# A two-layer decoder on one core: causal maxima and turned rows of maxima leave the place between a step's two pairs of scores

## What is computed

```
scale = 1.0 / sqrt(16)
q = heads(x @ Wq + bq);  k = heads(x @ Wk + bk);  v = heads(x @ Wv + bv)
att = where(causal, einsum('bhqd,bhkd->bhqk', q, k) * scale, -inf)
y = einsum('bhqk,bhkd->bhqd', softmax(att), v)
qc = heads(x @ Wcq + bcq);  kc = heads(ctx @ Wck + bck);  vc = heads(ctx @ Wcv + bcv)
y = y + einsum('bhqk,bhkd->bhqd', softmax(einsum('bhqd,bhkd->bhqk', qc, kc) * scale), vc)
return y @ Wp + bp
```

## Time and profile before

| | |
|---|---|
| time, median of 3 runs | 1605.59 us (1604.62 to 1607.55) |
| span of the profiled execution, first to last instruction | 1608.6 us |
| PE busy | 1504.9 us, 94% of the span |
| DVE, ACT, POOL busy | 871.6, 712.0, 571.8 us |
| steps of `xa` | 301 to 585 us |
| steps of `a1` | 889 to 1030 us |
| steps of `a2` | 1147 to 1380 us |

### The profile page before, as it was taken

The page is one execution under the profiler, slowest core; times in us unless marked ns, Lnnn a source line. Parts: engine busy times, 40 slices in busy tenths (PEclk is TensorE's granted clock), DMA queues, the critical chain, the costliest instruction groups (busy, mean ns, idle before and its releaser), DMA issues.

```text
span 1608.6 us, 24316 instructions
## 1 busy us (share of the span) xinstructions
PE 1504.9 (94%) x9774; PEld 818.2 (51%) x9774; DVE 871.6 (54%) x1838; ACT 712.0 (44%) x1035; POOL 571.8 (36%) x637
## 2 busy tenths in 40 slices
PE   7999999999999996997899999998899999998997
PEld 4678863333333353694553333564233333567997
DVE  3256538888888636204673567435677775213221
ACT  4544323366656644432334455443355556432331
POOL 3043225622222211403021355431367778613211
PEclk9999999999999998999999799999799999998999
DMA  6000020000000007972300000130200000190200
GB/s 208 1 1 1 1 50 7 1 1 1 1 1 1 1 1 261 318 246 62 40 21 1 1 1 2 53 118 29 96 2 1 2 1 27 65 348 31 97 12 9
DMA packets 70531, 85.29 MB, mean 53 GB/s; under 512 B 25008, under 2 KB 55953, under 8 KB 69266
## 3 DMA queue, kind: packets, MB, share of 16 engines
q1 hardware_dynamic: 67585, 76.35, 14.8%
q0 software_dynamic: 2832, 7.38, 1.4%
HBM read 64.60 MB, written 19.51 MB: 52 GB/s over the span
## 4 chain that ended last, share of the span: by engine, by line
PE 83%; DVE 8%; DMA 3%; ACT 3%; issue 1%; SPq 1%; POOL 1%; DVEq 0%; POOLq 0%; ACTq 0%
PE psum L1383 14%; PE psum L1402 10%; PE psum L1348 6%; PE psum L3487 5%; PE psum L700 4%; PE psum L2755 3%; PE psum L2746 3%; PE psum L1424 3%; PE psum L1550 3%; DVE a_nm L1475 2%; PE psum L3498 2%; PE psum L2270 2%; PE psum L368 2%; PE psum L740 2%; PE psum L1584 2%; PE psum L2724 2%
## 5 line engine op out<-in xcount | busy, mean ns | idle before, releaser
L1475 DVE TENSOR_REDUCE a_nm<-psum 128x1 f32<-128x512 f32 x384 | 250.6, 685 | 130.7 <-PE psum L1348 90.0
L1475 DVE TENSOR_REDUCE xa_nm<-psum 128x1 f32<-128x512 f32 x256 | 161.6, 680 | 22.1 <-PE psum L1348 18.8
L1437 ACT ACTIVATE xnT<-psum 128x1024 f32<-128x1024 f32 (+1 forms) x104 | 95.2, 960 | 60.6 <-PE psum L1383 55.5
L1437 ACT ACTIVATE a_w<-psum 128x1024 f32<-128x1024 f32 x86 | 83.8, 1022 | 69.1 <-PE psum L1383 59.1
L1383 PE MATMUL psum<-xa_cq,ctxT 32*128 32x512 f32 x512 | 113.4, 635 | 0.8 <-ACT xn L1437 0.8
L1383 PE MATMUL psum<-a2qT,a2kT 32*128 32x512 f32 x512 | 98.0, 608 | 0.0
L1348 PE MATMUL psum<-a2kr,a2qr 32*128 32x512 bf16 x256 | 84.3, 396 | 13.8 <-DVE a_nm L1475 13.1
L1348 PEld LDWEIGHTS psum<-a2kr,a2qr 32*128 32x128 bf16 x256 | 21.0, 91 | 121.8 <-DVE a_nm L1475 109.7
L1437 ACT ACTIVATE xn<-psum 128x1024 f32<-128x1024 f32 (+1 forms) x64 | 59.5, 971 | 39.2 <-PE psum L1383 39.1
L1348 PE MATMUL psum<-xa_ckr,xa_cqr 32*128 32x512 bf16 x256 | 69.1, 382 | 6.7 <-DVE xa_nm L1475 6.3
L1379 PE MATMUL psum<-a_mrow,onesb 3*128 3x512 bf16 x384 | 70.0, 399 | 1.4 <-DVE a_mrow L1503 1.1
(11 more groups left out here) (553 smaller groups left out, 3370.9 us busy)
## 6 DMA issues: line engine op xcount, KB each, us to landing
mo_w<-in_L_ffn_W SPq DMA_DIRECT2D x14, 1024.0 KB, 7.6
sw_wv<-in_L_ffn_w_v SPq DMA_DIRECT2D x4, 2048.0 KB, 18.7
scratch_a2v<-co_stages SPq DMA_DIRECT2D x16, 256.0 KB, 2.1
scratch_a2k<-co_stages SPq DMA_DIRECT2D x16, 256.0 KB, 3.6
a2kT<-scratch_a2k SPq DMA_DIRECT2D x8, 512.0 KB, 8.2
a2v<-scratch_a2v SPq DMA_DIRECT2D x4, 1024.0 KB, 11.9
sw_wp<-in_L_ffn_w_proj SPq DMA_DIRECT2D x4, 1024.0 KB, 19.2
a1li<-in_L_xattn_a_li_w SPq DMA_DIRECT2D x2, 1024.0 KB, 6.3
```

Of the source, the lines that this page charges most:

```text
L1437: e.activation(self.weights(n, c)[:, 2 * jj:2 * jj + 2, lo:S], ps[:, pr:pr + 2, lo:S], ACT.Exp, scale=self.scale).then_inc(*self.weighed.m ...
L1475: e.tensor_reduce(self.nm[n % 3][:, q, part, h:h + 1], view, AX.X, ALU.max, negate=True).then_inc(*self.max_taken.mark(*i))
```

## The change

`spread` no longer lets every item go to place 1. Only a "max" of a job that isn't causal may still stand there; a causal "max" and every "max_rows" start at place 2.

```diff
@@ -1152,7 +1152,8 @@
         for j, step in enumerate(given):
-            place = min(range(1, len(times)), key=lambda p: abs(times[p] - (j + 0.6) * times[-1] / len(given)) + 0.5 * len(spread[p]))
+            narrow = step[0] == "max" and self.jobs[step[1][0]].mode != "causal"
+            place = min(range(1 if narrow else 2, len(times)), key=lambda p: abs(times[p] - (j + 0.6) * times[-1] / len(given)) + 0.5 * len(spread[p]))
             if step[0] == "max":
```

## The result

| | before | changed |
|---|---|---|
| median | 1606.53 us (1604.62 to 1607.55, 4 runs) | 1588.7 us (1584.82 to 1592.6, 4 runs) |
| ratio | | 0.9876, 95% interval 0.9856 to 0.9896 |
| profiled execution | 1608.6 us | 1583.1 us |
| mean granted clock of it | 0.965 | 0.961 |

What follows compares the result with a forecast made beforehand. PE's own list was taken as the bound. `xa` saves 24.8 - 3.7 = 21.1 us and `a1` 3.0, together 24.1: 1605.6 - 24.1 = 1581.5 us, own range 1577 to 1587, 8-in-10 range 1576 to 1592.

Steps and rivals of the forecast that it cites:

- The barrier and its price: Full-width split steps of `xa`: moving all-row work from between the pairs saves 1.16 us each, one pair (1.06) and one change (0.1).
- ACT's exponential takes the barrier's place: Rival, changed steps of `xa`: pair 1 keeps waiting for ACT, 11.0 us given back, 1588.8 us; 12 in 100.
- four heads slower than two: Rival, scores of split steps: four heads together take 0.32 us a step more than the trace shows, 1587.9 us; 7 in 100.
- DVE and the ring: Rival, 20 steps: DVE or the ring of three banks becomes the bound, 0.69 us waited in each, 1595.3 us; 4 in 100.
- The late second pair: `xa`: pair 1 waits for banks until ACT's second exponential of the step before; at (4,3) this costs 0.84 us.
- The other first steps and (2,3): `xa`, first steps of the other runs of changed steps, and (2,3): pair 1 late, 0.9 us given back together.
- The ends of the runs: `xa`, behind the shortened last step of each of seven runs of changed steps: later waits give back 2.0 us.
- the rule: `xa`: behind a step of length P, pair 1 is late by 3.16 - P us, and the step is longer by that.
- the narrow steps: `xa`, steps (11,2) with 256 queries and (13,1) with 384: they save 0.6 and 0.95 us, together 1.6.
- `a1`: Five split steps of `a1`: scores to values take 1.84 us in place of 2.47; 0.6 saved a step, 3.0 in all.
- So nothing is counted for them.: `a2`, DMA, the other four engines and later stages: order unchanged, later stages only start earlier, so no saving or loss was counted.
- The rival on the clock: Rival: PE waits more between steps, `xa` is granted `a1`'s mean clock of 0.90, and the kernel takes 1610 us; 3 in 100.

## Why the prediction was right, and where it was off

- **The barrier and its price.** 1.16 us a full-width step was forecast; 15 of the 20 saved 1.15 to 1.19, by the starts of the score matmuls in the two traces, and step (4,4) came out at 3.80 for a sum of 3.82. The rival that ACT's exponential takes the barrier's place, that of four heads slower than two, and that of DVE and the ring are out: the eight matmuls take 1.14, and PE's idle waits for DVE in `xa` are 3.8 us, and for ACT 0.8, as before. By the estimate from the page that was cited, the Trainium skill (TensorE: Matmul & The Clock Gate, Measured speedup vs the span model), `xa` would have saved 6.4 us less; the measured rows decide against it for these matmuls.
- **The late second pair.** (4,3) saved 0.33 for a forecast 1.16 - 0.84 = 0.32. The other first steps and (2,3) gave back 1.1 for an estimate of 0.9.
- **The ends of the runs**, which were to give back 2.0: the term of the sum that was too large. The steps behind grew by 0.28 in all, 0.14 in two of them. Behind a step of 2.83 pair 1 is 0.33 late by the rule, but the next step begins with two or three maxima of 32 rows and a wait for DVE of its own, under which the lateness hides. With the narrow steps (0.46 and 0.93 for 0.6 and 0.95) `xa` saves 22.3 for 21.1.
- **`a1`.** 5 x 0.39 = 2.0 for 3.0. The step of the argument that failed is taking the 1.19 of an unsplit step for the scores; they took 1.46. That step followed one of 6.12 us. Behind the 2.84 us ahead of the changed steps, pair 1 waits for ACT's second exponential. The prediction counted this wait for `xa` and left it out for `a1`.
- **"So nothing is counted for them."** This is what the median missed. The steps' sum is 24.3 us for 24.1. By the medians 6.5 us of it were missing in the first comparison and 0.7 and 3.9 on two other chips; on the last the total gained 1.3 more. The profiles of two chips show a loss between `a1` and `a2`, through the clock; what the executions without a profile lost, and where, isn't shown. The forecast's own range, 1577 to 1587, missed the first median by 1.7 us; the wide one held it. The rival on the clock had the mechanism and the wrong place: `xa` stayed at 1.00, the stages behind it didn't.
- **What was luck.** The steps' sum meets the forecast to 0.2 us because two sizes that were off cancel: `xa` gave 1.2 more than forecast, `a1` 1.0 less. And the first median, 1588.7, lies beside the 1588.8 of the rival in which pair 1 keeps waiting for ACT. The match says nothing for it: that rival takes the loss from `xa`, which saved more than was forecast.

## What to carry to other kernels

Matmuls of 32 rows each, on different rows, run together here only while nothing of all 128 rows stands between them in PE's list. Put work of all rows in one group at one place of a step, and put work of few rows between the pairs, where it is free. Count a wait that such a barrier had covered: it comes back, as at (4,3) and in `a1`. And where PE's clock comes and goes, judge a change by the lengths of its stages in several profiles, not by one median: here `xa`'s steps repeat to 0.1 us in seven of eight profiles while the totals of one kernel spread over 21.

## What was not expected

The mean granted clock of one kernel on one chip ran from 0.947 to 0.964 with times of 1603.2 to 1581.7 us, and a kernel that was shortened by 24 us at full clock showed a lower mean on each chip where both were read (0.958 for 0.960, 0.9585 for 0.966, 0.9635 for 0.966); only about 0.0005 of that is the same low time in a shorter span. The kernel before takes 1606.5 to 1610.1 us on three chips and 1626 to 1628 on two others. It was profiled on two of the three, with `xa`'s steps the same to 0.1 us. The profiles of the changed kernel say where the 20 us lie: on one of the slower chips `xa`'s steps take the same, while the stage from `xa` to `a1` takes 315.9 us for 308.2 and the one behind `a2`'s last step 243.2 for 230.7, at granted clocks of 0.91 for 0.93 and 0.93 for 0.96. PE is busy for 7.1 us more of these 20.2 and idle for the rest; why, no run here tells.
